# GpSimd sums a head group's probabilities over the key tiles off the diagonal

## What is computed

```python
q = rmsnorm(rope(h @ Wq.T), w_qn)          # 16 heads of 32
k = rmsnorm(rope(h @ Wk.T), w_kn)          # one head, shared
v = h @ Wv.T                               # one head, shared
scores = einsum('bhqd,bkd->bhqk', q, k) * hd ** -0.5
attn = softmax(where(causal, scores, min)) # exp(s - max) / sum over the keys
out = einsum('bhqk,bkd->bhqd', attn, v)
```

## Time and profile before

| | us |
|---|---|
| median of 3 runs | 1260.75 |
| lowest, highest | 1259.95, 1263.04 |
| the profiled execution, its own time | 1264.72 |
| its span, first to last instruction | 1262.9 |
| PE, DVE, ACT, POOL busy in it | 1149.0, 990.5, 753.4, 495.3 |
| mean granted clock of PE, share of full | 0.962 |

### The profile page before, as it was taken

How to read it: one execution, slowest core, us unless ns; L and a number is a source line. 1 busy time by engine, 2 the same in 40 slices (tenths; PEclk the granted TensorE clock), 3 DMA queues, 4 the chain that set the end, 5 groups by cost and what they waited for, 6 DMA issues and landing times.

```text
span 1262.9 us, 25455 instructions
## 1 busy us (share of the span) xinstructions
PE 1149.0 (91%) x8828; PEld 875.0 (69%) x8828; DVE 990.5 (78%) x1903; ACT 753.4 (60%) x1497; POOL 495.3 (39%) x375
## 2 busy tenths in 40 slices
PE   8989999999998888999897999999999999999940
PEld 4545556555565655555556989999999999999930
DVE  4678786766548888685567798999999989999968
ACT  3456555556665434555644367787777778787720
POOL 1213211121122212011010127878878887887740
PEclk9999999989999879999999999999999999999975
DMA  9570000000000000002014149999999999999968
GB/s 351 175 277 1 1 18 2 9 10 2 22 2 9 10 13 10 1 21 83 22 42 133 55 149 267 297 300 300 298 297 298 299 296 299 298 300 298 295 176 282
DMA packets 77166, 189.93 MB, mean 150 GB/s; under 512 B 11496, under 2 KB 12136, under 8 KB 76832
## 3 DMA queue, kind: packets, MB, share of 16 engines
q1 hardware_dynamic: 44256, 112.01, 26.1%
q0 software_dynamic: 28672, 71.32, 23.2%
q10 hardware_dynamic: 4160, 5.58, 1.2%
HBM read 136.36 MB, written 52.51 MB: 150 GB/s over the span
## 4 chain that ended last, share of the span: by engine, by line
PE 63%; DVE 14%; DMA 6%; issue 5%; DVEq 5%; POOL 4%; ACT 3%; POOLq 0%; SPq 0%; ACTq 0%
PE ps L1249 17%; PE ps L1288 9%; PE ps L1070 8%; PE ps L1055 4%; PE ps L1098 4%; PE ps L991 4%; PE ps L1023 4%; DMA acc_dram<-y,slots 4%; PE ps L1235 3%; DVE nmax L1491 3%; POOL acc_dram L665 3%; PE ps L1040 2%; PE ps L963 1%; PE ps L1085 1%; POOL xg L650 1%
## 5 line engine op out<-in xcount | busy, mean ns | idle before, releaser
L665 POOL DMA_INDIRECT acc_dram<-y,slots x128 | 250.0, 1953 | 80.2 <-issue 48.6
L1491 DVE TENSOR_REDUCE nmax<-ps 128x1 f32<-128x512 f32 (+3 forms) x304 | 191.6, 657 | 94.5 <-PE ps L1027 53.2
L774 ACT ACTIVATE probs<-ps 128x512 f32<-128x512 f32 (+1 forms) x320 | 159.2, 554 | 88.1 <-PE ps L1055 87.0
L616 POOL TENSOR_SCALAR_AFFINE_SELECT probs<-probs 128x512 f32<-128x512 f32 x64 | 44.4, 695 | 382.1 <-ACT probs L774 382.0
L650 POOL DMA_INDIRECT xg<-h_dram,slots x128 | 129.5, 1012 | 107.5 <-DVE slots L1682 49.1
L1023 PE MATMUL ps<-kpad,qpT 128*128 128x512 f32 (+3 forms) x384 | 148.5, 455 | 13.6 <-DVE nmax L1491 11.6
L1249 PE MATMUL ps<-x_hi,e_gu_hi 128*112 128x256 f32 (+1 forms) x768 | 120.1, 278 | 0.0
L1249 PE MATMUL ps<-x_hi,e_gu_lo 128*112 128x256 f32 (+1 forms) x768 | 119.6, 278 | 0.0
L1055 PE MATMUL ps<-qT,kT 98*128 98x512 f32 (+1 forms) x320 | 114.6, 436 | 5.0 <-ACT probs L774 4.8
L1249 PE MATMUL ps<-x_lo,e_gu_hi 128*112 128x256 f32 (+1 forms) x768 | 110.2, 279 | 1.5 <-DVE x_lo L1693 1.2
L1693 DVE TENSOR_TENSOR e_gu_lo<-e_gu,e_gu_hi 128x1408 fp32r<-128x1408 f32 x64 | 104.0, 1624 | 8.8 <-issue 6.0
(11 more groups left out here) (222 smaller groups left out, 2361.4 us busy)
## 6 DMA issues: line engine op xcount, KB each, us to landing
e_gu<-in_gate_up SPq DMA_DIRECT2D x64, 704.0 KB
e_d<-in_w_down SPq DMA_DIRECT2D x64, 224.0 KB
acc_dram<-h SPq DMA_DIRECT2D x2, 4608.0 KB, 25.8
e_d<-in_w_down SPq DMA_DIRECT2D x64, 128.0 KB
wmod_b<-in_wmod SPq DMA_DIRECT2D x2, 2048.0 KB, 22.1
xg<-h_dram SPq DMA_DIRECT2D x16, 256.0 KB, 3.3
acc_a<-acc_dram SPq DMA_DIRECT2D x8, 512.0 KB, 11.5
acc_b<-acc_dram SPq DMA_DIRECT2D x8, 512.0 KB, 7.5
```

The lines of the kernel that those rows point to most:

```text
L665: pool.indirect_dma_start(out=acc_dram[a], out_offset=bass.IndirectOffsetOnAxis(ap=slots[:, at:at + 1], axis=0), in_=y[e % 2][:, h, :], in ...
L774: act.activation(probs[:, n % PROBS, 2 * pr:2 * pr + 2, off:CW], unit_bank(2 * n + pr)[:, :, off:CW], ACT.Exp).then_inc(s_exp, 1)
L1491: dve.tensor_reduce(nmax[:, 1 if lo else 0, first:first + heads], max_view(n, heads, hi - lo), AX.X, ALU.max, negate=True).then_inc(s_max, 1)
```

## The change

part_sum, a buffer of 128 x 4 x 256, is added. In chunks with K = 4, 6 or 8 key tiles POOL adds the probabilities of tiles 0 and 1, then adds each further tile off the diagonal to the sum (add_probs, tiles 1 to K-3). values leaves out the products of these tiles with ones and forms one product of part_sum with ones instead, at the group's last pair; the two tiles on the diagonal keep theirs (DIRECT = 2). A semaphore s_sum counts the additions; values waits for it, and so does exponentials before it overwrites a tile that POOL still has to read. add_probs stands behind the other parts of its slot on POOL.

To make room, sq now lies in the same memory as xn, with waits in normalise (s_rope) and squares (s_xT), and squares moves from -22 to -20; scratch is gone, and mean_square and residual write h2 in its place, with the waits that shift had before.

```diff
 PROBS = 4
+DIRECT = 2
...
-        xn = sb(att, "xn", [P, D])
+        xn_sq = sb(att, "xn_sq", [P, H + 1, HD])
+        xn, sq = xn_sq[:, 0:H, :].rearrange("p h d -> p (h d)"), xn_sq
...
-        sq = sb(att, "sq", [P, H + 1, HD])
...
-        scratch = sb(att, "scratch", [P, D])
+        part_sum = sb(att, "part_sum", [P, GH, CW])
...
+        all_steps = [(q, g, kt) for q in range(NCHUNK) for g in range(NG) for kt in range(keys(q))]
+
...
+        def added(q):
+
+            return max(0, keys(q) - 1 - DIRECT)
+
+        def sums_to(q, g, kt):
+
+            return sum(NG * added(k) for k in range(q)) + g * added(q) + min(kt, added(q))
...
-              "key_value_out": -27, "query_out": -23, "squares": -22, "rotate": -15, "head_rms": -11, "split": -9,
+              "key_value_out": -27, "query_out": -23, "squares": -20, "rotate": -15, "head_rms": -11, "split": -9,
...
+            def add_probs(q, g, kt):
+                n = step_of(q, g, kt)
+                if kt == 1:
+                    pool.wait_ge(s_pv, (n - 1) // 2)
+                pool.wait_ge(s_exp, 2 * n + 2)
+                pool.drain()
+                before = probs[:, (n - 1) % PROBS, :, :] if kt == 1 else part_sum[:, :, :]
+                pool.tensor_tensor(part_sum[:, :, :], before, probs[:, n % PROBS, :, :], ALU.add).then_inc(s_sum, 1)
...
+                for q, g, kt in steps_at(m):
+                    if 1 <= kt <= added(q):
+                        add_probs(q, g, kt)
...
+                if t >= 2:
+                    act.wait_ge(s_rope, t - 1)
...
+                act.wait_ge(s_xT, min(t + 2, NT))
...
                     act.wait_ge(s_pv, (n - PROBS) // 2 + 1)
+                    q0, g0, kt0 = all_steps[n - PROBS]
+                    if kt0 <= added(q0) and added(q0):
+                        act.wait_ge(s_sum, sums_to(q0, g0, max(kt0, 1)))
...
-                for at in (0, CW):
-                    for kt in (2 * k, 2 * k + 1):
-                        off = first_query(q, kt)
-                        for j in range(GH):
-                            last = pe.matmul(ps[HD * j:HD * j + HD, PV_BANK, at + off:at + CW],
-                                             v_sb[:, b, kt, :] if at == 0 else ones[:, :],
-                                             probs[:, (n + kt % 2) % PROBS, j, off:CW], start=(kt == 0 and at == 0),
-                                             stop=(kt == keys(q) - 1 and at == CW))
+                for kt in (2 * k, 2 * k + 1):
+                    off = first_query(q, kt)
+                    for j in range(GH):
+                        last = pe.matmul(ps[HD * j:HD * j + HD, PV_BANK, off:CW], v_sb[:, b, kt, :],
+                                         probs[:, (n + kt % 2) % PROBS, j, off:CW], start=(kt == 0), stop=False)
+                if k == last_pair and added(q):
+                    pe.wait_ge(s_sum, sums_to(q, g, added(q)))
+                    for j in range(GH):
+                        pe.matmul(ps[HD * j:HD * j + HD, PV_BANK, CW:2 * CW], ones[:, :], part_sum[:, j, :], start=False, stop=False)
+                for kt in (2 * k, 2 * k + 1):
+                    if added(q) and kt <= added(q):
+                        continue
+                    off = first_query(q, kt)
+                    for j in range(GH):
+                        last = pe.matmul(ps[HD * j:HD * j + HD, PV_BANK, CW + off:2 * CW], ones[:, :],
+                                         probs[:, (n + kt % 2) % PROBS, j, off:CW], start=False, stop=(kt == keys(q) - 1))
...
+                if q == 0:
+                    dve.wait_ge(s_init, 48)
+                else:
+                    dve.wait_ge(s_h2_out[0], 16 * q)
+                    dve.wait_ge(s_h2t, CT * q - 1)
                 for j in range(CT):
-                    dve.tensor_tensor_reduce(scratch[:, j * P:(j + 1) * P], ps[:, gram_bank(q), j * P:(j + 1) * P], ident, 1.0, 0.0,
+                    dve.tensor_tensor_reduce(h2[:, 0, j * P:(j + 1) * P], ps[:, gram_bank(q), j * P:(j + 1) * P], ident, 1.0, 0.0,
...
+                    if t >= 2:
+                        dve.wait_ge(s_h2_out[slot], 16 * (t // 2))
+                        dve.wait_ge(s_h2t, t - 1)
+                    scratch = h2[:, slot, :]
...
```

More of the change, by code:

```diff
@@ L275, in build_program @@
         s_kv, s_kve, s_exr, s_posr = (sem("s_" + n) for n in ("kv", "kve", "exr", "posr"))
-        s_gb = sem("s_gb")
+        s_gb, s_sum = sem("s_gb"), sem("s_sum")
         s_pack_k, s_qp = sem("s_pack_k"), sem("s_qp")
@@ L722, in normalise @@
                     act.wait_ge(s_xT, t)
-                act.activation(xn[:, :], xtile(t), ACT.Identity, bias=center[:, t:t + 1], scale=rstd[:, t:t + 1])\
+                if t >= 2:
+                    act.wait_ge(s_rope, t - 1)
+                act.activation(xn, xtile(t), ACT.Identity, bias=center[:, t:t + 1], scale=rstd[:, t:t + 1])\
                    .then_inc(s_xn, 1)
@@ L1527, in residual @@
                     dve.wait_ge(s_at, t + 1)
-                    dve.scalar_tensor_tensor(scratch[:, :], ps[:, tile_bank(t), :], orstd[:, q % 2, j:j + 1], ga[:, t // TPB, :],
+                    if t >= 2:
+                        dve.wait_ge(s_h2_out[slot], 16 * (t // 2))
+                        dve.wait_ge(s_h2t, t - 1)
+                    scratch = h2[:, slot, :]
+                    dve.scalar_tensor_tensor(scratch, ps[:, tile_bank(t), :], orstd[:, q % 2, j:j + 1], ga[:, t // TPB, :],
                                              ALU.mult, ALU.mult).then_inc(s_atd, 1)
                     dve.drain()
-                    dve.tensor_tensor(xt, xt, scratch[:, :], ALU.add)
+                    dve.tensor_tensor(xt, xt, scratch, ALU.add)
                 else:
@@ L1542, in shift @@
                 dve.wait_ge(s_rstd2, t + 1)
[L1543 to L1547, removed]
                 dve.scalar_tensor_tensor(row, xtile(t), mv2[:, slot, 0:1], cscale[:, b, :], ALU.subtract, ALU.mult)
```

## The result

| | median us | runs | ratio to before, 95% interval |
|---|---|---|---|
| kernel before | 1261.89 | 4 | |
| changed kernel | 1339.46 (1337.91 to 1341.75) | 4 | 1.061 [1.058, 1.064] |

The profiled execution has a span of 1338.0 us against 1262.9, so 75.1 us have to be found. PE's products with ones did go: 704 records instead of 1280. Yet the time grew by 77.6 us where 8.7 were forecast. The first view is the page of the changed kernel, its line of busy times and the granted clock in 40 slices.

What follows compares the result with a forecast made beforehand. PE was taken to set the attention's pace, DVE a close second. Chunk terms -1 - 3 - 1.5 + 2 - 3 + 15.2 gave +8.7 us, from 1260.75 to 1269.5 us; eight in ten: 1238 to 1288.

Steps and rivals of the forecast that it cites:

- PE's saving, 33.5 us: Chunks 1-3 and 5-7: PE drops the ones products of 72 key tiles; if PE alone decided, the gain is 33.5 us.
- The length of an addition: On POOL, one addition of 128x1024 f32 takes 2.24 us, midway between 1.94 and 2.54; 72 take 161 us.
- The queue at the port in chunk 7, 82 us: Chunk 7: DVE's port work, 20 additions, 8 selects and handovers queue for 82 us against a 66.7 us stretch: +15.2 us.
- Chunks 2, 3 and 6: "room": DVE's idle time leaves room for additions in chunks 2 and 6, -3 us each; chunk 3's port queue nearly fits, -1.5.
- Chunk 5 and chunk 1: Four additions each: +2 us in chunk 5, where DVE is at 87%; -1 in chunk 1, where DVE idles 12.6 us.
- The other edits, nothing: Later squares, normalise's waits and scratch moved into h2 wait only for things several slots old, so they cost nothing.
- Rival 4, POOL's own round: Mainly chunk 7: additions, selects and PE's last pair form a round where POOL sets the pace; up to +30, 1291 us; 20%.
- The remark on the clock: PE starved by POOL's round may also be granted less clock; chunk 5, where it waits most, has 0.87.
- Whose reading of the port: At the shared SBUF port, a DVE instruction with two SBUF inputs stands still until POOL's instruction finishes; PSUM-reading row maxima are spared.

## Why the prediction was wrong

The direction and the mechanism were right: DVE's two-input instructions stand still behind POOL's reads, chunk 7 pays most, the row maxima are spared. The size was off by a factor of nine, because the stops were priced as a queue at the port and as room in DVE's idle time, and not as time added to DVE's steps on the path. By the steps of the prediction:

- **PE's saving, 33.5 us.** The work went as counted. Alone it is worth 17.7 us, and 0.3 in chunk 7. What failed here is reading PE's 93% busy there as PE setting the pace; it moved no term of the sum, but it hid that the chain of chunk 7 already had 26.6 us on DVE, with no slack for a stop. The view of waits of that stretch in the kernel before, which I did not use, points the same way (who waited for whom, us in total, times, longest us):

```profile
ACT probs L774 <- PE ps L1055: 16.1, 14, 3.3
DVE biased L1568 <- ACT ex L801: 12.8, 2, 9.4
...
PE ps L1149 <- ACT hot_row L816: 3.6, 1, 3.6
ACT hot_row L816 <- DVE hot_row L1665: 3.5, 1, 3.5
```

  PE waits for ACT, ACT for DVE, DVE for ACT, ACT for PE. My reading is that an engine that is busy inside such a ring need not be its bound; what is measured is the 0.3 us.
- **The length of an addition.** 2.24 forecast, 2.34 undisturbed, 2.43 in the mean. The estimate from the Trainium skill, "GPSIMD Engine Reference", section Elementwise — side-by-side cycle accounting, 2.25, is as near. Not the fault.
- **The queue at the port in chunk 7, 82 us.** With 2.34 in place of 2.24 it is 84; the stretch measured 100. A sum of all users' times is what the port needs if someone always stands in line. Here both sides have pauses: in that stretch POOL waits 15.0 us for PE's last pair (L1109) and 8.8 for exponentials before its additions, DVE 12.0 for ACT's ex. The stop itself, not the port's total, goes onto the path: DVE +36.6 us, the chain's DVE part +32.4, stretch +33.4. This step, +15.2 for what was +33.4, missed 18 us.
- **Chunks 2, 3 and 6: "room".** This is the step with the largest miss, 7.5 us of gain forecast and 32.3 of loss measured, 40 of the 61 us by which the stretches missed the sum; here the direction was wrong too. Two errors. First, DVE's waiting was never summed: the additions cost DVE 16.3, 30.2 and 12.7 us, 1.1 to 1.5 each. Second, DVE's idle time was taken to absorb it. Against the run with PE's saving alone, these stretches are 11.0, 21.9 and 12.8 us longer, 77% of what DVE waited; 4.7 of these 45.7 us are there with the powers too. Idle time that is spread between dependent steps covered little here; with 12 additions in chunk 3 instead of 20 it covered half or more.
- **Chunk 5 and chunk 1.** +2.5 and +2.9 measured, +2 and -1 forecast: right in chunk 5, wrong in direction in chunk 1.
- **The other edits, nothing.** They cost 5 us, without a reason found.
- **Rival 4, POOL's own round.** It exists, but small: with a power in place of the addition, chunk 7 is 71.0 us against 66.6, its chain has 12.5 us on POOL, and over the whole run PE waits 9.3 us for the masks behind the powers. Of the 18.4 us between the two spans 8.4 lie before the end of chunk 7 and 10 behind it. POOL's time explains that run's 15.4 us, not the 73. The remark on the clock held: granted 0.80 in chunk 7, where PE now waits for DVE, 0.97 before. What it costs was not separated; PE has 148 records fewer in the stretch and is busy for 60.6 us instead of 61.8. On the chain of that stretch PE's part did not grow: 26.5 us, 28.9 before.
- **Whose reading of the port.** The Trainium skill, "SBUF — State Buffer", section Who interferes with whom, says that two-input DVE instructions contend with GpSimd instructions that read, not with those that only write. The trace agrees: 785 ns under additions, 444 under fills. Its sentence that the pair is held for the whole instruction stands there of DVE's 2-port modes; the prediction took it for two-input instructions as well. Read so, it fits the additions (longest stops 2.62, 1.54, 0.97 us) but not the power, which runs for 2.43 us and leaves DVE at 443 ns, and its cast at 428.

In numbers, as a chain of medians: 1263 before, +5 for making room, -18 for PE, +15 for POOL's time and waits, +73 for the additions' use of SBUF: 1339 (rounded; each step from one kernel to the next).

## What to carry to other kernels

Before giving POOL elementwise work, count DVE's instructions with two SBUF inputs in the same stretch (and its casts and scalar operations, which were held too), not DVE's busy share: each addition of 2.34 us cost DVE 1.1 to 1.8 us of waiting in chunks 2, 3, 6 and 7, 0.7 and 1.1 in chunks 1 and 5. In chunk 7, where such instructions lie on the chain, nearly all of it arrived. Take the price per stop, the length of the POOL instruction that is met, and expect idle time between dependent steps to absorb only a part of it, the less the denser the additions are; shorter POOL instructions shorten the stops until POOL's own time runs out. And check that PE's busy share in a stretch is its bound: removing work from it as a blank experiment shows this at once.

## What the runs showed of the hardware that was not expected

- DVE and POOL can fall into turns, one instruction each. A DVE instruction on 32 elements took 2.46 us beside an addition of 2.45; hot_col and hot_row, 0.4 us each, took 2.6 us three times in a row from 683.3 us on.
- A POOL product of a tile with itself takes 1.89 us for 1024 elements, an addition of two different tiles 2.34; whether the operation or the shared input makes the difference is not shown. Additions of 256, 512 and 1024 elements take 0.71, 1.25 and 2.34 us undisturbed: 2.1 ns an element and about 0.2 us fixed.
- A POOL power of 13 columns, 2.43 us, leaves DVE's two-input instructions and its casts alone (443 and 428 ns). POOL fills leave the two-input instructions alone but lengthen DVE's casts in SBUF (433 to 545 ns); additions lengthen both (443 to 785 and 433 to 709 ns).
